# The last column of each state's scan: copied by VectorE instead of ScalarE

## The chip, the core and the metric

The kernel runs on one core of a Trainium2 chip. A core has five engines that run side by side, each with its own queue of instructions: TensorE (PE, matrix products), VectorE (DVE), ScalarE (ACT), GpSimd (POOL) and SyncE (SP, which starts transfers). They wait for each other through semaphores. An instruction that waits holds up everything behind it in its own queue. The metric is the time of one execution on the device in microseconds (us); lower is better.

## The reference

The input x has shape (2, 2048, 256): two sequences of 2048 tokens. Two blocks follow each other, each added to its input. The first is a Mamba block with a gated feed-forward part, the second a mixture of eight low-rank experts, two for each token. What matters here is the selective scan in the Mamba block. For each of 512 channels d and each of 16 states s:

```python
dA = jnp.exp(dt_t[..., None] * A)
h = h * dA + dt_t[..., None] * B_t[:, None, :] * x_t[..., None]
y = jnp.einsum('bds,bs->bd', h, C_t)
```

h starts at zero and runs on through all 2048 tokens. The output y goes through a gate and a projection. A kernel that cuts the tokens into chunks must hand h at the last token of a chunk to the same sequence's next chunk.

## The kernel before

The tokens are cut into 8 chunks of 256 for each of the 2 sequences, so there are 16 **steps**, written (chunk, sequence). The 512 channels lie on 128 partitions as 4 blocks. In a step the 16 **states** go round one after the other, and each state's scan has two **parts** of two channel blocks (a "pair" of scans, 128x256 each).

For a state s the engines do this:

- ScalarE makes the decays dA with four exponentials (L871) and, for most states, the weighted inputs bxT (L859). GpSimd makes bxT for states 4, 6 and 8 (L602).
- TensorE turns bxT into one of three PSUM banks psx (L1340), one bank for each pair. It must wait until the pair that used the bank three fills earlier has been scanned.
- VectorE scans: two instructions for each part (L1095). It reads dA and psx, starts from the column `state[:, b, j, s]`, and writes h, a ring of three states. The last two states, 14 and 15, have their decays in PSUM (L882) and their inputs in SBUF.
- GpSimd multiplies h by C into hC (L631), one instruction of 128x1024 for each state, after both parts.
- TensorE sums the states into psy (L1359).
- ScalarE copies the last column of h into `state` (L889), for the same sequence's next chunk. This is `keep_state`. A later scan that writes the same slot of the ring waits for it (`state_saved`).

Around these lies the rest of the network. `drive` sets the order on every engine: for each state s first `main(s, n, 0)`, then the stage work of turn s of other steps (`enter` and `ready` prepare the coming steps, `back` and `tail` finish earlier ones), then `main(s, n, 1)`. So up to five steps are in work at once, and VectorE's stage work (convolution taps L1059, softplus repair L1067 to L1073, sums out of PSUM L1111, L1133 and L1189, gates L1126, expert weights L1170, router L1149 to L1159) stands between the first and the second pair of a state, while a second pair and the next state's first pair follow each other directly. In `drive`:

```python
for s in range(S):
    if n:
        main(s, n, 0)
    for name in order[s] if s in order else order["else"]:
        ...
    if n:
        main(s, n, 1)
```

ScalarE issues `keep_state(s - 1, n)` in `main(s, n, 1)`, ahead of bxT and the decays of state s + 3, and `keep_state(15)` in the first turn of `back`.

Of the kernel before, what the change touches and what calls it, by code (L numbers as in the profile page):

```python
# [6 lines left out]
B, L, DM, DI, S, TAPS, DTR, HID = 2, 2048, 256, 512, 16, 4, 128, 1024  # L7
NE, RANK = 8, 128
P = 128
T = 256  # L10
# [10 lines left out]
HALVES = 2  # L21
PAIR = NJ // HALVES
FILLS = S * HALVES
# [34 lines left out]
def count(per_step, step, k):  # L58

    c, b = step  # L60
    value = c * (2 * per_step) + (per_step * b + k)
    return max(value, 0) if isinstance(value, int) else value
# [51 lines left out]
def ring(s):  # L114

    return s % 3 if s < S - 1 else 1
# [81 lines left out]
def mamba_moe(nc, x, params, w_in, w_x, w_dt, w_out, w_ff, w_fo, w_a, w_b, w_r, bc_scratch, cw_scratch, out):  # L198
    f32 = mybir.dt.float32
    ALU = mybir.AluOpType  # L200
    ACT = mybir.ActivationFunctionType
# [6 lines left out]
    with ctx:  # L208
        def sb(name, shape):
            return ctx.enter_context(nc.sbuf_tensor(name, shape, f32))  # L210
# [56 lines left out]
        h = sb("h", [P, 3, NJ, T])  # L267
        hC = sb("hC", [P, RC, NJ, T])
        state = sb("state", [P, B, NJ, S])
# [78 lines left out]
        exp_done, scan_done, state_saved = sem("exp_done"), sem("scan_done"), sem("state_saved")  # L348
# [341 lines left out]
        def _(act):  # L690
# [192 lines left out]
                                                scale=neg_a[:, j, s:s + 1])  # L883
                last.then_inc(direct_exp, 1)

            def keep_state(s, n):

                act.wait_ge(scan_done, count(FILLS, n, HALVES * (s + 1)))
                nc.scalar.activation(state[:, n[1], :, s:s + 1], h[:, ring(s), :, T - 1:T], ACT.Copy  # L889
                                     ).then_inc(state_saved, 1)  # L890

            def gate(i, m):

                act.wait_ge(filled_back, back_fill(f"G{i}", m))
# [2 lines left out]
            def main(s, n, part):  # L897
                if s + 1 in DIRECT:
                    decay_direct(s + 1, part, n)
                if part == 0 and s == 3:  # L900
                    act.wait_ge(yg_done, count(2, n, -2))
                    act.wait_ge(z0_filled, count(1, n, 1))
                    nc.scalar.activation(sz[:, n[1], 0, :], psb[:, :, :].rearrange("p k t -> p (k t)"), ACT.Copy
                                         ).then_inc(z0_copied, 1)
                if part == 1:
                    if s > 0:
                        keep_state(s - 1, n)
                    if s == 10:
                        act.wait_ge(z0_copied, count(1, n, 1))
                        act.wait_ge(z1_copied, count(1, n, 1))  # L910
                        nc.scalar.activation(sz[:, n[1]], sz[:, n[1]], ACT.Silu).then_inc(sz_done, 1)
                        if not is_first(n):
                            gate(1, prev(n))
                        use_log_exp()
                    made(s, n)

            def back(s, m):
                if s == 0:
                    keep_state(S - 1, m)
                if s in (3, 4):  # L920

                    i = s - 3
                    act.wait_ge(filled_back, back_fill(f"YG{i}", m))
                    nc.scalar.activation(yg[:, 2 * i:2 * i + 2, :], (psb, pst)[i][:, :, :], ACT.Copy).then_inc(yg_moved, 1)  # L924
                if s == 7:
                    act.wait_ge(stats[1], count(1, m, 1))
                    inv_std(2, mv[1][:, :, 1], m).then_inc(rstd_done[2], 1)
                    if not is_last(m):
                        mean_shift(1, m)
                        act.wait_ge(cw_done, count(1, m, 0))  # L930
                        normalise(1, nx, x1, vn_done)
                if s == 9:

                    act.wait_ge(filled_back, back_fill("vT", m))
                    act.wait_ge(filled_dt, count(len(DT_UNITS), m, 2 if is_late(m) else 2 * len(DT_UNITS) + 2))
                    act.wait_ge(cw_stored, count(16, m, 0))
                    for k in range(KM):
                        last = nc.scalar.activation(nT[:, k, :], psb[:, k, :], ACT.Identity, scale=pcol(C_LN2W + k),  # L938
                                                    bias=pcol(C_LN2B + k))
                    last.then_inc(vT_done, 1)  # L940
                if s == 10:
                    gate(0, m)
                    if is_last(m):
                        gate(1, m)
                        use_log_exp()
                if s == 15:
                    act.wait_ge(stats[2], count(1, m, 1))
                    inv_std(3, mv[2][:, :, 1], m).then_inc(rstd_done[3], 1)
                    if not is_last(m):
                        mean_shift(2, m)  # L950
                        act.wait_ge(filled_back, back_fill("vT", m))
                        normalise(2, nx, x2[:, m[1]], xe_done)
# [36 lines left out]
        def _(dve):  # L989
# [85 lines left out]
            def main(s, n, part):  # L1075
                b, r = n[1], ring(s)
                fill = HALVES * s + part
                if part == 0:
                    if s in DIRECT:
                        dve.wait_ge(direct_done, count(ND, n, s - DIRECT[0] + 1))  # L1080
                    else:
                        dve.wait_ge(exp_done, count(S - ND, n, s + 1))

                    dve.wait_ge(hc_done, count(S, n, ring_before(s) + 1))
                    dve.wait_ge(state_saved, count(S, n, ring_before(s) + 1))
                if s in DIRECT:
                    dve.wait_ge(direct_exp, count(HALVES * ND, n, fill - TURNED + 1))
                else:
                    dve.wait_ge(bx_filled, count(TURNED, n, fill + 1))
                for k in range(PAIR):  # L1090
                    j = PAIR * part + k
                    in_psum = psx[bx_bank(fill)][:, k, :]
                    decays, inputs = ((in_psum, direct_inputs(s)[:, j, :]) if s in DIRECT
                                      else (dA[:, s % RA, j, :], in_psum))
                    last = nc.vector.tensor_tensor_scan(h[:, r, j, :], decays, inputs, state[:, b, j, s:s + 1],  # L1095
                                                        ALU.mult, ALU.add)
                last.then_inc(scan_done, 1)

            def back(s, m):
                b = m[1]  # L1100
                if s == 2:

                    dve.wait_ge(y_summed, count(S, m, S))
                    dve.wait_ge(sz_done, count(1, m, 1))
                    for j in range(SUB):
                        nc.vector.tensor_tensor(ygt[:, j, :], psy[j][:, :], sz[:, b, j, :], ALU.mult).then_inc(yg_done, 1)
                if s == 6:

                    dve.wait_ge(filled_back, back_fill("op", m))
                    dve.wait_ge(xk_copied, count(16, m, 16))  # L1110
                    nc.vector.tensor_tensor(x1[:, :, :], xk[:, b], psb[:, :, :], ALU.add).then_inc(x1_done, 1)  # L1111
                    dve.wait_ge(x1_done, count(1, m, 1))
                    norm_stats(1, x1, "back", m)
                if s == 7 and is_last(m):
                    dve.wait_ge(cw_done, count(1, m, 0))
                    dve.wait_ge(rstd_done[2], count(1, m, 1))
                    normalise(1, nx, x1, vn_done)
                if s == 15 and is_last(m):
                    dve.wait_ge(filled_back, back_fill("vT", m))
                    dve.wait_ge(rstd_done[3], count(1, m, 1))  # L1120
                    normalise(2, nx, x2[:, b], xe_done)
                if s in (11, 12):
                    i = s - 11
                    dve.wait_ge(gate_done, count(2, m, i + 1))
                    dve.wait_ge(filled_back, back_fill(f"A{i}", m))
                    nc.vector.tensor_tensor(hg[:, 2 * i:2 * i + 2, :], hg[:, 2 * i:2 * i + 2, :],  # L1126
                                            up_bank(i, m)[:, :, :], ALU.mult).then_inc(hg_done, 1)
                if s == 14:

                    dve.wait_ge(filled_back, back_fill("fo", m))  # L1130
                    dve.wait_ge(x1x_done, count(1, m, 1))
                    dve.wait_ge(out_stored, count(16, m, -16))
                    nc.vector.tensor_tensor(x2[:, b], xb[:, :, :], psb[:, :, :], ALU.add).then_inc(x2_done, 1)  # L1133
                    dve.wait_ge(x2_done, count(1, m, 1))
                    norm_stats(2, x2[:, b], "back", m)
# [406 lines left out]
```

## Time and profile before

| | |
|---|---|
| three runs, median (lowest to highest) | 1285.68 us (1285.03 to 1286.23) |
| the profiled execution | 1286.74 us |
| its span, from the first instruction to the last | 1284.8 us |
| granted TensorE clock, mean of the span | 0.979 |
| PE, DVE, ACT, POOL busy | 93%, 77%, 85%, 79% of the span |

The busy share is an average over the span. In the opening and in the last stretch some engines have little to do; in between, TensorE's share is higher than 93%. An engine's idle time is shown with what released it. A wait for several semaphores is put down to the last one.

### The profile page before, as it was taken

To read this page: it belongs to the slowest core of one execution; us is meant where nothing else is said; L and a number is where in the kernel's file an instruction comes from. 1 tells how busy PE (TensorE), PEld (TensorE's weight loads), DVE (VectorE), ACT (ScalarE), POOL (GpSimd) and SP (SyncE) were. 2 spreads that over 40 slices of the span, in tenths; PEclk is the share of its full clock that TensorE was granted. 3 is DMA by queue.
4 is the path that set the end of the run, shared out by engine and by line. 5 is a ranking of instruction groups with operands and counts; after the bars stand their busy time and mean duration, and the time that the engine had idled before them with its cause. 6 is when DMAs were issued, how large, how long until landed. Compare 5 with 4: busy or idle time off the path is not lost.

```text
span 1284.8 us, 24309 instructions
## 1 busy us (share of the span) xinstructions
PE 1197.1 (93%) x7422; PEld 1029.2 (80%) x7422; DVE 995.6 (77%) x1800; ACT 1089.1 (85%) x2656; POOL 1019.4 (79%) x760
## 2 busy tenths in 40 slices
PE   5677989999999999999999999999999999998988
PEld 3466778888888888888888888888888888787876
DVE  2587987889797887879788887978889796887733
ACT  4888999899898989989898998989899998988621
POOL 2489798888888988888898888889888887888621
PEclk8797999999999999999999999999999999999999
DMA  2511102112221312222121222213121221203010
GB/s 69 199 58 52 65 19 105 46 52 90 67 92 34 100 43 64 79 68 91 42 94 43 69 72 69 92 36 98 43 75 67 68 83 53 87 36 99 17 50 17
DMA packets 33927, 86.83 MB, mean 68 GB/s; under 512 B 3592, under 2 KB 16512, under 8 KB 31360
## 3 DMA queue, kind: packets, MB, share of 16 engines
q1 hardware_dynamic: 33792, 85.20, 20.2%
q8 instruction: 64, 1.05, 0.3%
q14 instruction: 71, 0.58, 0.1%
HBM read 67.76 MB, written 4.84 MB: 57 GB/s over the span
## 4 chain that ended last, share of the span: by engine, by line
PE 67%; DVE 8%; issue 4%; ACT 2%; POOL 2%; DMA 2%; DVEq 0%; SPq 0%; ACTq 0%; POOLq 0%
PE psy L1359 11%; PE psx L1340 10%; PE pst L1220 8%; PE psb L1220 7%; PE psb L1214 6%; PE psf L1214 5%; PE pst L1214 4%; DVE h L1095 4%; PE psf L1308 2%; PE psf L1314 2%; PE psf L1258 2%; PE psf L1247 2%; PE psb L1314 2%; DVE acc L1059 2%; PE psb L1207 1%
## 5 line engine op out<-in xcount | busy, mean ns | idle before, releaser
L631 POOL TENSOR_TENSOR hC<-h,bC 128x1024 f32<-128x1024 f32 x256 | 604.5, 2368 | 126.1 <-DVE h L1095 116.8
L1095 DVE TENSOR_TENSOR_SCAN h<-dA,state,psx 128x256 f32<-128x256 f32 x896 | 597.2, 726 | 102.3 <-PE psx L1340 94.4
L871 ACT ACTIVATE dA<-dt,neg_a 128x256 f32<-128x256 f32 x896 | 380.1, 500 | 0.0
L1340 PE MATMUL psx<-ident,bxT 128*128 128x128 f32 x1792 | 270.5, 278 | 34.1 <-DVE h L1095 28.7
L1340 PEld LDWEIGHTS psx<-ident,bxT 128*128 128x128 f32 x1792 | 215.7, 143 | 74.4 <-issue 29.6
L1359 PE MATMUL psy<-ident,hC 128*128 128x128 f32 x2048 | 267.7, 274 | 3.9 <-POOL hC L631 3.9
L1359 PEld LDWEIGHTS psy<-ident,hC 128*128 128x128 f32 x2048 | 235.7, 142 | 10.6 <-POOL hC L631 4.7
L859 ACT ACTIVATE bxT<-uTs,BT 128x512 f32<-128x512 f32 x352 | 232.4, 715 | 5.9 <-PE psx L1340 3.1
L1220 PE MATMUL pst<-w_b_sb,cbc 128*128 128x256 f32 x480 | 110.8, 379 | 0.0
L1220 PEld LDWEIGHTS pst<-w_b_sb,cbc 128*128 128x128 f32 x480 | 90.1, 190 | 11.7
L882 ACT ACTIVATE psx<-dt,neg_a 128x256 f32<-128x256 f32 x128 | 55.3, 463 | 49.7 <-DVE h L1095 49.7
L602 POOL TENSOR_TENSOR bxT<-uTs,BT 128x1024 f32<-128x1024 f32 x48 | 91.2, 1899 | 4.4 <-PE psx L1340 4.3
L1214 PE MATMUL psb<-nT,w_ff_sb 128*128 128x256 f32 x376 | 91.7, 387 | 1.4 <-ACT nT L938 1.4
L1059 DVE SCALAR_TENSOR_TENSOR acc<-psf,par,acc 128x255 f32<-128x255 f32 (+1 forms) x180 | 73.9, 474 | 24.6 <-ACT halo L763 24.6
L1214 PEld LDWEIGHTS psb<-nT,w_ff_sb 128*128 128x128 f32 x376 | 68.9, 190 | 15.5 <-issue 5.7
L1214 PE MATMUL pst<-eT,w_a_sb 128*128 128x256 f32 x336 | 80.7, 384 | 0.0
L1214 PEld LDWEIGHTS pst<-eT,w_a_sb 128*128 128x128 f32 x336 | 62.6, 193 | 7.6
L1214 PE MATMUL psf<-uT,w_in_sb 128*128 128x256 f32 x240 | 60.7, 397 | 4.1 <-ACT uT L748 2.1
L1220 PE MATMUL psb<-w_out_sb,yg 128*128 128x256 f32 x256 | 62.0, 385 | 2.0 <-ACT yg L924 2.0
L1220 PE MATMUL psb<-w_fo_sb,yg 128*128 128x256 f32 x256 | 60.4, 379 | 0.0
L590 POOL TENSOR_TENSOR dt<-dt,sp_l 128x1024 f32<-128x1024 f32 x16 | 37.8, 2360 | 28.0 <-DVE sp_l L1073 28.0
L1095 DVE TENSOR_TENSOR_SCAN h<-psx,state,sp_e 128x256 f32<-128x256 f32 x64 | 44.2, 735 | 17.1 <-ACT state L889 12.8
(178 smaller groups left out, 1894.5 us busy)
## 6 DMA issues: line engine op xcount, KB each, us to landing
bC<-bc_scratch SPq DMA_DIRECT2D x64, 512.0 KB, 4.0
cbc<-cw_scratch SPq DMA_DIRECT2D x15, 1024.0 KB, 4.7
uk<-sp_l SPq DMA_DIRECT2D x16, 512.0 KB, 6.3
xf<-in_x SPq DMA_DIRECT2D x16, 256.0 KB, 2.7
xk<-xn SPq DMA_DIRECT2D x16, 256.0 KB, 4.3
un<-bc_scratch SPq DMA_DIRECT2D x16, 256.0 KB, 4.1
xb<-in_x SPq DMA_DIRECT2D x16, 256.0 KB, 5.3
out<-x SPq DMA_DIRECT2D x16, 256.0 KB, 2.2
```

The costliest lines, as they stand in the source:

```text
L602: nc.gpsimd.tensor_tensor(bxT[:, s % RX], uTs[:, n[1]], BT[:, n[1], :, s:s + 1].to_broadcast([P, SUB, DI]), ALU.mult).then_inc(bxT_pool, 1)
L631: nc.gpsimd.tensor_tensor(hC[:, s % RC], h[:, ring(s)], bC[:, g % RINGG, s % G:s % G + 1, :].to_broadcast([P, NJ, T]), ALU.mult).then_inc( ...
L859: last = nc.scalar.activation(bxT[:, s % RX, j, :], uTs[:, n[1], j, :], ACT.Copy, scale=BT[:, n[1], j, s:s + 1])
L871: last = nc.scalar.activation(dA[:, s % RA, j, :], dt[:, n[1], j, :], ACT.Exp, scale=neg_a[:, j, s:s + 1])
L882: last = nc.scalar.activation(psx[bx_bank(fill)][:, k, :], dt[:, n[1], j, :], ACT.Exp, scale=neg_a[:, j, s:s + 1])
L1059: nc.vector.scalar_tensor_tensor(out=acc[:, j, tap:], in0=x_bank(i, m)[:, j % 2, 0:T - tap], scalar=pcol(C_CONVW + j * TAPS + k), in1=acc[ ...
L1095: last = nc.vector.tensor_tensor_scan(h[:, r, j, :], decays, inputs, state[:, b, j, s:s + 1], ALU.mult, ALU.add)
L1214: last = mm(dst[:, i, :], w[:, k, c:c + P], rhs[:, k, :], start=k == 0, stop=k == kt - 1)
L1220: last = mm(dst[:, j, :], lhs[:, k, j * P:(j + 1) * P], w[:, k, :], start=k == 0, stop=k == kt - 1)
L1314: last = mm(dst[:, :, :].rearrange("p k t -> p (k t)"), uT[:, b, k, j * P:(j + 1) * P], w_in_sb[:, k, DI:2 * DI], start=k == 0, stop=k == ...
L1340: last = nc.tensor.transpose(psx[bx_bank(fill)][:, k, j * P:(j + 1) * P], bxT[:, s % RX, j, c:c + P], ident[:, :])
L1359: last = mm(psy[j][:, i * P:(i + 1) * P], hC[:, s % RC, i, j * P:(j + 1) * P], ident[:, :], is_transpose=True, start=False, stop=s == S - ...
```

## The change

ScalarE no longer copies the last column. VectorE does, with `tensor_copy` in place of an activation: the copy of state s - 1 stands behind the first pair of scans of state s, and that of state 15 in the first turn of `back`, behind the first pair of state 0 of the next step. It waits on VectorE's own semaphore `scan_done` for the second pair of its state. The scans still wait for `state_saved`, which VectorE now raises itself.

```diff
 # ScalarE
-            def keep_state(s, n):
-
-                act.wait_ge(scan_done, count(FILLS, n, HALVES * (s + 1)))
-                nc.scalar.activation(state[:, n[1], :, s:s + 1], h[:, ring(s), :, T - 1:T], ACT.Copy
-                                     ).then_inc(state_saved, 1)
...
                 if part == 1:
-                    if s > 0:
-                        keep_state(s - 1, n)
...
             def back(s, m):
-                if s == 0:
-                    keep_state(S - 1, m)
...
 # VectorE, main
                 last.then_inc(scan_done, 1)
+                if part == 0 and s > 0:
+                    keep_state(s - 1, n)
+
+            def keep_state(s, n):
+
+                dve.wait_ge(scan_done, count(FILLS, n, HALVES * (s + 1)))
+                nc.vector.tensor_copy(state[:, n[1], :, s:s + 1], h[:, ring(s), :, T - 1:T]).then_inc(state_saved, 1)
 
             def back(s, m):
                 b = m[1]
+                if s == 0:
+                    keep_state(S - 1, m)
```

VectorE's queue before, from the second pair of state 7 to the second pair of state 8 (the listing calls the scans SCALAR_TENSOR_TENSOR; psx0 to psx2 are the banks, and [waits ...] are the semaphores an instruction waits for):

```order
L1095 SCALAR_TENSOR_TENSOR h<-dA,state,psx0 128x256 [waits bx_filled]
L1095 SCALAR_TENSOR_TENSOR h<-dA,state,psx0 128x256
L1095 SCALAR_TENSOR_TENSOR h<-dA,state,psx1 128x256 [waits state_saved,bx_filled,hc_done,exp_done]
L1095 SCALAR_TENSOR_TENSOR h<-dA,state,psx1 128x256
L1170 TENSOR_TENSOR cbc<-cbc,psb 128x512 [waits filled_tail]
L1067 SCALAR_TENSOR_TENSOR sp_l<-sp_l,ln_one,sp_e 128x1024 [waits sp_ln]
L1069 TENSOR_SCALAR sp_e<-sp_e 128x1024
L1095 SCALAR_TENSOR_TENSOR h<-dA,state,psx2 128x256 [waits bx_filled]
```

The same place in the changed kernel, whose lines are numbered up to ten lower:

```order
L1085 SCALAR_TENSOR_TENSOR h<-dA,state,psx0 128x256 [waits bx_filled]
L1085 SCALAR_TENSOR_TENSOR h<-dA,state,psx0 128x256
L1085 SCALAR_TENSOR_TENSOR h<-dA,state,psx1 128x256 [waits state_saved,bx_filled,hc_done,exp_done]
L1085 SCALAR_TENSOR_TENSOR h<-dA,state,psx1 128x256
L1094 COPY state<-h 128x4 [waits scan_done]
L1169 TENSOR_TENSOR cbc<-cbc,psb 128x512 [waits filled_tail]
L1057 SCALAR_TENSOR_TENSOR sp_l<-sp_l,ln_one,sp_e 128x1024 [waits sp_ln]
L1059 TENSOR_SCALAR sp_e<-sp_e 128x1024
L1085 SCALAR_TENSOR_TENSOR h<-dA,state,psx2 128x256 [waits bx_filled]
```

The copy of state 7 now stands between state 8's first pair and the stage work of that turn; the rest keeps its order.

ScalarE's queue before, in turns 7 and 8 of a step (sz is a half of the gate, copied out of PSUM):

```order
L889 ACTIVATE state<-h 128x4 [waits scan_done]
L859 ACTIVATE bxT<-uTs,BT 128x512 [waits bx_filled]
L859 ACTIVATE bxT<-uTs,BT 128x512
L871 ACTIVATE dA<-dt,neg_a 128x256 [waits scan_done]
L871 ACTIVATE dA<-dt,neg_a 128x256 x3
L818 ACTIVATE sz<-psf 128x512 [waits filled_dt,yg_done]
```

The same place in the changed kernel:

```order
L859 ACTIVATE bxT<-uTs,BT 128x512 [waits bx_filled]
L859 ACTIVATE bxT<-uTs,BT 128x512
L871 ACTIVATE dA<-dt,neg_a 128x256 [waits scan_done]
L871 ACTIVATE dA<-dt,neg_a 128x256 x3
L818 ACTIVATE sz<-psf 128x512 [waits filled_dt,yg_done]
```

The copy and its wait for the scans ahead of bxT are gone; the decays behind bxT wait for the same scans as before.

## Rows read from the trace of the kernel before

**Rows 1.** The page's first part: busy us (share of the span) xinstructions.

```profile
PE 1197.1 (93%) x7422; PEld 1029.2 (80%) x7422; DVE 995.6 (77%) x1800; ACT 1089.1 (85%) x2656; POOL 1019.4 (79%) x760
```

**Rows 2.** Busy us in five stretches: PE, PEld, DVE, ACT, POOL; clock, DMA, GB/s.

```profile
48.65:119.00 70.35, 50.65 (x291) 40.26 (x288) 52.97 (x86) 64.76 (x154) 56.31 (x34) 0.84 0.16 50
119.00:188.90 69.90, 61.60 (x387) 51.79 (x387) 58.61 (x101) 62.98 (x155) 61.12 (x35) 0.94 0.17 54
188.90:1084.76 895.86, 878.76 (x5568) 761.38 (x5568) 738.57 (x1328) 809.97 (x1991) 763.26 (x563) 1.00 0.21 68
1084.76:1154.66 69.90, 66.90 (x436) 59.17 (x436) 55.81 (x96) 62.56 (x153) 57.81 (x37) 1.00 0.22 69
1154.66:1224.30 69.64, 63.11 (x415) 56.57 (x416) 53.27 (x92) 48.27 (x121) 53.22 (x35) 0.98 0.19 58
```

**Rows 3.** VectorE's waits, 188.90 to 1084.76: us in total, times, longest.

```profile
DVE h L1095 <- PE psx L1340: 69.8, 47, 3.3
DVE yg L1126 <- PE psb L1214: 26.3, 13, 2.3
DVE x L1111 <- PE psb L1220: 14.9, 12, 1.2
DVE acc L1059 <- ACT halo L763: 12.5, 12, 1.2
DVE h L1095 <- ACT state L889: 10.4, 12, 0.9
DVE x L1189 <- PE pst L1220: 8.8, 12, 0.8
```

**Rows 4.** TensorE's waits in the same stretch.

```profile
PE psx L1340 <- DVE h L1095: 9.3, 12, 0.8
...
PE psx L1340 <- ACT bxT L859: 2.5, 2, 1.3
```

**Rows 5.** One line's instructions: xcount, ns min/median/max, first and last start.

```profile
L889 ACT ACTIVATE state<-h x256: 192/195/243, 60.3 to 1224.3; 128x4 f32<-128x4 f32 x128
```

**Rows 6.** The same view of four VectorE lines.

```profile
L1154 DVE TENSOR_TENSOR lgm<-lg,mx x16: 174/386/1761, 201.8 to 1267.9; 128x16 f32<-128x16 f32 x16
...
L1159 DVE RECIPROCAL rden<-den x16: 166/166/167, 207.5 to 1273.0; 128x2 f32<-128x2 f32 x16
...
L1069 DVE TENSOR_SCALAR sp_e<-sp_e x16: 679/680/687, 35.0 to 1122.2; 128x1024 f32<-128x1024 f32 x16
...
L1073 DVE TENSOR_TENSOR sp_l<-sp_l,sp_e x16: 1225/1898/2328, 35.7 to 1126.0; 128x1024 f32<-128x1024 f32 x16
```

**Rows 7.** Timeline, VectorE then GpSimd: start us, us, engine, line, operation, [idle before].

```profile
1162.92 1.76 DVE L1154 TENSOR_TENSOR lgm<-lg,mx 128x16 f32<-128x16 f32 x1
...
1162.29 2.35 POOL L631 TENSOR_TENSOR hC<-h,bC 128x1024 f32<-128x1024 f32 x1
```

**Rows 8.** Timeline of VectorE in the step from 638.59 us.

```profile
645.11 2.66 DVE L1095 TENSOR_TENSOR_SCAN h<-dA,state,psx 128x256 f32<-128x256 f32 x4 [1.23 <-PE psx L1340]
...
649.45 0.18 DVE L1154 TENSOR_TENSOR lgm<-lg,mx 128x16 f32<-128x16 f32 x1
649.55 5.45 DVE L1095 TENSOR_TENSOR_SCAN h<-dA,state,psx 128x256 f32<-128x256 f32 x8
...
676.38 1.85 DVE L1067 SCALAR_TENSOR_TENSOR sp_l<-sp_l,ln_one,sp_e 128x1024 f32<-128x1024 f32 x1
...
678.75 2.65 DVE L1095 TENSOR_TENSOR_SCAN h<-dA,state,psx 128x256 f32<-128x256 f32 x4
```

**Rows 9.** Timeline of GpSimd in the same step.

```profile
647.01 2.38 POOL L631 TENSOR_TENSOR hC<-h,bC 128x1024 f32<-128x1024 f32 x1
...
654.88 2.36 POOL L631 TENSOR_TENSOR hC<-h,bC 128x1024 f32<-128x1024 f32 x1
...
674.77 2.38 POOL L631 TENSOR_TENSOR hC<-h,bC 128x1024 f32<-128x1024 f32 x1 [0.34 <-DVE h L1095]
680.36 2.36 POOL L631 TENSOR_TENSOR hC<-h,bC 128x1024 f32<-128x1024 f32 x1 [3.21 <-DVE h L1095]
```

## The prediction

> **What bounds the kernel now.** I read the page's busy line first. It shows TensorE busy for 93% of the span and GpSimd, ScalarE and VectorE for 77 to 85% [rows 1]. Then the windows, cut where the first scan of a step starts. There are 16 steps, of 16 states each. The 12 steps from 188.90 to 1084.76 us take 895.86 us, so 74.7 us each. TensorE is busy for 878.76 of that (98%), VectorE for 738.57 (61.5 a step), ScalarE for 809.97 and GpSimd for 763.26 (63.6 a step) [rows 2]. So in the steady part TensorE sets the pace, at full clock, and VectorE has 74.7 - 61.5 = 13.2 us of idle time in a step. The waits say where that idle time is: VectorE waits for TensorE's psx banks (69.8 us over the 12 steps), for the gate halves, out_proj and the expert sum (26.3, 14.9 and 8.8), for ScalarE's halo (12.5) and for ScalarE's saved state (10.4) [rows 3]. TensorE in turn waits little: 9.3 us for scans and 2.5 us for ScalarE's bxT [rows 4].
>
> **What is removed.** ScalarE loses 256 copies of 195 ns [rows 5]. It is not the bound, and the only one who waits for them is the first scan of state 15, 12 times in 12 steps, 0.87 us each [rows 3]. That wait goes. What is late next there is the sum L1189, which waits for TensorE [rows 3], so the end of the step does not come earlier. ScalarE's decays still wait for the scans of the state before. The stalls of TensorE on bxT, 2.5 us in all [rows 4], are the most that a freer ScalarE can give back. I take zero for the removal, with 2.5 us as its bound.
>
> **What is added.** VectorE gets 256 copies of 128x4, SBUF to SBUF, 16 a step, each behind the first pair of scans of the next state. The wait on the own scan costs nothing: that scan ended a whole pair of scans (half of 2.66 us for four, 1.33 us) earlier. What the copy itself costs no row shows, because VectorE has no copy in this trace. The nearest rows disagree:
>
> Cheap end: the reciprocal L1159, one SBUF input, 128x2, takes 166 to 167 ns in all 16 cases [rows 6], and a short instruction of this kind takes 0.10 us of the queue: L1154 starts at 649.45 and the next scan at 649.55 [rows 8]. So 16 x 0.10 = 1.6 us a step, inside 13.2 us of idle time.
>
> Dear end: L1154, a 128x16 subtraction with two SBUF inputs, takes 174 ns at least and up to 1761 ns [rows 6]. In that longest case it starts at 1162.92 and ends at 1164.68, and GpSimd's product, begun at 1162.29, ends at 1164.64 [rows 7]. The subtraction stood until GpSimd's instruction was over. L1067 does the same: begun at 676.38 for 1.85 us, while GpSimd's product runs from 674.77 to 677.15 [rows 8, 9], which is 0.77 us of standing and 1.08 of work. So a VectorE instruction that needs a second way into SBUF waits for whatever GpSimd is running.
>
> Is the copy of that sort? L1069, with one SBUF input and an SBUF output, does 1024 elements in 0.68 us, where L1073 with two inputs needs 1.225 us at best [rows 6]. So it handles two elements at a time, which a single way in at L1073's pace would not feed. It never meets GpSimd in this trace: it stands between L1067 and the next scans, when GpSimd idles until 680.36 for a scan [rows 8, 9]. I take the copy to be of L1069's sort, with L1154's wait, and not of the reciprocal's.
>
> A rule speaks against this change here. The Trainium skill's page SBUF — State Buffer, section Who interferes with whom, says that copies and tensor_scalar can run in a two-port mode, that the second port pair is shared with GpSimd, and that whichever issues first holds it for its whole instruction while the other blocks. Its list of such operations is copy, cast and tensor_scalar; the reciprocal is not in it. By that rule the sum below holds, and by the reciprocal's row alone it would be 1286. The waits in [rows 7] agree with the rule for two inputs; that a copy behaves so no run here shows yet.
>
> **The price of a wait.** The copy stands behind the first pair of state s, and at that moment GpSimd is usually inside the product of state s-1, which began when that state's second pair ended. Read in one step (from 638.59 us): the four scans from 678.75 end at 681.41 while GpSimd's product ends at 682.72: 1.32 us left. Those from 645.11 end at 647.77 and the product at 649.39: 1.6 us. The eight from 649.55 end at 655.00 and the product at 657.24: 2.2 us [rows 8, 9]. Over the 16 places of that step, read in the same way, the rests are 0, 0.65, 1.61, 0, 2.24, 0.35, 0.82, 1.25, 1.26, 1.32, 0.03, 0.61, 2.10, 1.43, 1.24 and 0.25, together 15.2 us. When VectorE becomes the slower one, most places turn into the plain case of 1.25 (product of 2.37 less the pair of 1.33, and a start that lags a little), which makes 16 x 1.25 = 20. I take 17.5.
>
> The sum of VectorE for one steady step: 61.5 busy, less 1.8 of waits for GpSimd that are in it already and that the copy ahead now takes over (0.77 at L1067, 0.8 at L1073, 0.2 at L1154, median less minimum in [rows 6] for the last), plus 17.5 of waiting, plus 1.6 for the copies: 78.8. That is more than the 74.7 that TensorE needs, so VectorE becomes the bound. Its other idle time does not all go. Waits behind the copy in the queue (for the gate halves, out_proj, halo, expert sum and half of the psx waits) are covered by the standing time; the rest of the psx waits, about half of 69.8 / 12 = 5.8, stays: 3. So 81.8 us a step, 7.1 more, and 12 x 7.1 = 85 us. The four steps at the ends, by the same sum from their own busy time [rows 2]: the first 53.0 + 20.3 = 73.3 against 70.4, the second 78.9 against 69.9, the last two 76.1 and 73.6 against 69.9 and 69.6, together 22 us. The profiled execution took 1286.74 us; plus 107 that is 1394, and on the median of 1285.68, which is 1.06 lower, **1393 us**.
>
> What is queued behind the waiting copy: on VectorE the stage work of that state and the second pair of scans. For that pair wait GpSimd's product of the state and TensorE's next bank of psx, so TensorE is held up too.
>
> **Rivals.**
> 1. *The copy is of the reciprocal's sort.* It takes 1.6 us of 13.2 idle a step, nobody waits, and TensorE stays the bound. For it: L1159 never waited, and a copy of four elements has little use for two at a time. Against it: L1069's pace. Between 2.5 us off for the bxT stalls and some 3 us more where TensorE already waits for a scan (0.8 us at each of 12 step ends [rows 4], to which two copies add 0.2): 1283 to 1289, likeliest 1286, no change.
> 2. *The wait is there but hides.* With 15.2 us of rests and no idle time left, a step takes 61.5 - 1.8 + 15.2 + 1.6 = 76.5, 1.8 more: 12 x 1.8 plus some 5 at the ends, 1312 us. This is the low end of my own case.
> 3. *GpSimd's next instruction goes first.* If the copy stands until GpSimd has nothing left that is ready, the two engines overlap only in the first pair of each state: 63.6 of GpSimd, 1.6 of copies and 61.5 - 1.8 - 16 x 1.33 = 38.4 of the other VectorE work make 103.6 a step, 29 more, over 15 steps 1720 us at the far end. Half of it, 1500, if only some places have a next instruction ready. For it: GpSimd is busy for 63.6 of 74.7 us, so often something is ready. Against it: at L1067 and L1154 the waiting instruction went on as soon as the running one ended, though nothing was ready behind it there [rows 7 to 9], so the trace does not decide.
>
> The decision between 1 and the forecast falls at a wait of 13.2 / 16, about 0.7 us for each copy beyond its 0.1: under that VectorE's idle time holds it, above it the time grows.
>
> **How the numbers follow.** Forecast with its own range of 1312 to 1470 (high end: rests of 20 and 6 us of idle time left, 61.5 - 1.8 + 20 + 1.6 + 6 = 87.3, which is 12.6 more over 15 steps, 1475): 0.69, rival 2 in it. Rival 3: 0.14. Rival 1: 0.17, of which 0.05 faster, 0.09 no change, 0.03 a little slower. The likeliest is 1393. Leaving out rival 3 and the edges, 1284 to 1470 holds 8 in 10; it reaches to rival 1 because that is as likely as rival 3 and nearer. A measurement of this kernel can tell about 0.2% from no change, so faster 0.05, same 0.09, slower 0.86.
>
> **What would show it.** The copy's line in the profile after: a minimum near 0.1 and a median near 1.2 us shows the wait; a median under 0.2 us makes the forecast wrong and rival 1 right. In the windows, VectorE's busy time should rise from 61.5 to near 78 a step and TensorE's busy share fall from 98% to about 90%, with scans as what TensorE waits for. GpSimd's product should keep its 2.37 us. In the timelines each copy should end with GpSimd's running instruction; if it ends with the one after, it is rival 3. The wait of state 15 for ScalarE should be gone in every case.

## The result, and the profile after

The changed kernel takes 1385.92 us (median of 4 runs, 1382.47 to 1388.15), the kernel before beside it 1285.95 us (4 runs, 1285.03 to 1288.75). The ratio is 1.0778, with a 95% interval of 1.0752 to 1.0804: slower by 100 us, where the forecast was 1393 us. The profiled execution took 1388.15 us, with a span of 1386.2 us; the span is 101.4 us longer than before.

The page's first part for the changed kernel, with columns as in [rows 1]:

```profile
PE 1221.3 (88%) x7422; PEld 1040.1 (75%) x7422; DVE 1257.6 (91%) x2056; ACT 1066.4 (77%) x2400; POOL 1018.9 (74%) x760
```

VectorE has 256 instructions more and 262 us more of busy time, ScalarE 256 fewer and 22.7 us less. GpSimd's busy time is that of [rows 1]. VectorE is now the busiest engine. The chain of work that ended last, first by engine and then by line, says the same:

```profile
DVE 41%; PE 39%; issue 12%; ACT 4%; DVEq 1%; POOL 0%; ACTq 0%
DVE h L1085 20%; DVE state L1094 10%; PE psx L1339 6%; PE psb L1213 6%; PE psy L1358 5%; PE pst L1213 3%; DVE acc L1049 3%; PE psb L1219 3%; PE psf L1213 3%; PE pst L1219 2%; DVE bn L1002 2%; PE psf L1246 2%; ACT dA L871 1%; PE psf L1257 1%; DVE cbc L1169 1%
```

The new copy, `state` L1094, holds 10% of the chain. Next come the rows of single lines (name, count, ns min/median/max, first and last start): the copy, GpSimd's product, and three VectorE lines with two SBUF inputs, of which L1063 and L1153 are L1073 and L1154 of [rows 6], and L1057 is L1067 of [rows 8].

```profile
L1094 DVE COPY state<-h x256: 139/1354/2347, 54.8 to 1319.9; 128x4 f32<-128x4 f32 x128
...
L631 POOL TENSOR_TENSOR hC<-h,bC x256: 2339/2362/2393, 59.8 to 1319.9; 128x1024 f32<-128x1024 f32 x128
...
L1057 DVE SCALAR_TENSOR_TENSOR sp_l<-sp_l,ln_one,sp_e x16: 1271/1273/1284, 33.9 to 1208.5; 128x1024 f32<-128x1024 f32 x16
...
L1063 DVE TENSOR_TENSOR sp_l<-sp_l,sp_e x16: 1210/1212/1224, 35.8 to 1214.7; 128x1024 f32<-128x1024 f32 x16
...
L1153 DVE TENSOR_TENSOR lgm<-lg,mx x16: 174/175/641, 220.8 to 1366.6; 128x16 f32<-128x16 f32 x16
```

A copy of four elements takes 139 ns at best and 1354 in the median, ten times as long. GpSimd's product is as long as before. The three lines with two inputs no longer wait, one L1153 of 641 ns apart: the copy ahead of them has already stood until GpSimd's instruction was over. The timeline of one stretch shows it, VectorE first and then GpSimd (start us, us, engine, line, operation, [idle before]):

```profile
727.68 1.36 DVE L1085 TENSOR_TENSOR_SCAN h<-dA,state,psx 128x256 f32<-128x256 f32 x2
728.96 1.36 DVE L1094 COPY state<-h 128x4 f32<-128x4 f32 x1
730.23 0.68 DVE L1169 TENSOR_TENSOR cbc<-cbc,psb 128x512 f32<-128x512 f32 x1
730.83 1.27 DVE L1057 SCALAR_TENSOR_TENSOR sp_l<-sp_l,ln_one,sp_e 128x1024 f32<-128x1024 f32 x1
...
735.20 1.42 DVE L1094 COPY state<-h 128x4 f32<-128x4 f32 x1
...
740.83 0.14 DVE L1094 COPY state<-h 128x4 f32<-128x4 f32 x1
...
727.92 2.37 POOL L631 TENSOR_TENSOR hC<-h,bC 128x1024 f32<-128x1024 f32 x1 [1.62 <-DVE h L1085]
734.23 2.35 POOL L631 TENSOR_TENSOR hC<-h,bC 128x1024 f32<-128x1024 f32 x1 [3.94 <-DVE h L1085]
...
740.74 0.21 POOL L582 TENSOR_TENSOR acc<-acc,edge 128x12 f32<-128x12 f32 x1
```

The first copy starts at 728.96 and ends at 730.32; the product runs from 727.92 to 730.29. The second ends at 736.62, the product at 736.58. The third meets only a 0.21 us instruction and takes 0.14.

Where the 101.4 us are is read from the windows, cut as in [rows 2], with a sixth stretch for what follows the last scan:

```profile
48.71:126.14 77.43, 53.23 (x290) 41.78 (x288) 68.21 (x101) 64.46 (x141) 58.12 (x34) 0.79 0.15 46
126.14:206.26 80.12, 65.39 (x386) 54.91 (x386) 74.58 (x117) 62.46 (x140) 59.50 (x34) 0.88 0.15 47
206.26:1170.02 963.76, 887.98 (x5568) 761.68 (x5568) 932.36 (x1521) 791.29 (x1797) 762.53 (x562) 1.00 0.19 63
1170.02:1246.20 76.18, 67.60 (x436) 59.19 (x436) 75.14 (x111) 61.70 (x138) 57.81 (x37) 1.00 0.20 63
1246.20:1319.80 73.60, 64.51 (x418) 56.88 (x418) 70.52 (x108) 46.15 (x103) 53.18 (x35) 0.98 0.16 55
1319.80:1386.20 66.40, 55.39 (x238) 47.06 (x238) 19.96 (x57) 12.52 (x27) 12.04 (x28) 0.86 0.09 31
```

The 12 steady steps take 963.76 us instead of 895.86: 67.9 us, or 5.66 a step (80.3 against 74.7). VectorE is busy for 932.36 / 12 = 77.7 us of each and idle for 2.6; TensorE's share falls from 98% to 92%. The four steps at the ends take 7.1, 10.2, 6.3 and 4.0 us more, together 27.5. What follows the last scan takes 66.40 us instead of 60.50, so 5.9 more. The same stretch of the kernel before:

```profile
1224.30:1284.80 60.50, 48.83 (x244) 41.45 (x242) 19.66 (x55) 12.65 (x28) 12.04 (x28) 1.00 0.10 34
```

VectorE, ScalarE and GpSimd are as busy there as before; TensorE is busy for 55.39 us instead of 48.83, at a granted clock of 0.86 instead of 1.00. So these 5.9 us go with the clock and not with standing copies. The stretch up to the first scan gives the last 0.1.

What VectorE and TensorE wait for in the steady stretch (engine, line, releaser: us in total, times, longest):

```profile
DVE h L1085 <- PE psx L1339: 25.6, 23, 2.2
DVE x L1110 <- PE psb L1219: 1.4, 1, 1.4
...
PE psf L1213 <- DVE acc L1049: 21.3, 12, 2.0
PE psf L1313 <- DVE acc L1049: 17.8, 12, 1.5
PE psx L1339 <- DVE h L1085: 15.8, 25, 1.3
PE psb L1206 <- DVE cbc L1169: 8.5, 12, 0.7
```

VectorE's waits for the gate halves, out_proj, the expert sum, the halo and the saved state [rows 3] have shrunk to 1.4 us or are gone. Its waits for psx fell from 69.8 to 25.6 us. TensorE, which waited 9.3 us for scans [rows 4], now waits 63 us for VectorE's results in these four rows alone.

### The profile page after: what moved, and what is told of

Read it like the earlier page. It is cut to its first block, busy times and chain, and to the rows that moved or that the text cites. A ratio compares the mean times of both kernels' runs of the same rounds, so it can differ in the third digit from the quotient of the medians.

```text
span 1386.2 us, 24413 instructions
## 1 busy us (share of the span) xinstructions
PE 1221.3 (88%) x7422; PEld 1040.1 (75%) x7422; DVE 1257.6 (91%) x2056; ACT 1066.4 (77%) x2400; POOL 1018.9 (74%) x760
## 4 chain that ended last, share of the span: by engine, by line
DVE 41%; PE 39%; issue 12%; ACT 4%; DVEq 1%; POOL 0%; ACTq 0%
DVE h L1085 20%; DVE state L1094 10%; PE psx L1339 6%; PE psb L1213 6%; PE psy L1358 5%; PE pst L1213 3%; DVE acc L1049 3%; PE psb L1219 3%; PE psf L1213 3%; PE pst L1219 2%; DVE bn L1002 2%; PE psf L1246 2%; ACT dA L871 1%; PE psf L1257 1%; DVE cbc L1169 1%
## 5 line engine op out<-in xcount | busy, mean ns | idle before, releaser
L1094 DVE COPY state<-h 128x4 f32<-128x4 f32 x256 | 320.8, 1253 | 0.0
L1213 PE MATMUL psf<-uT,w_in_sb 128*128 128x256 f32 x240 | 63.7, 412 | 29.8 <-DVE acc L1049 27.7
L1213 PEld LDWEIGHTS psb<-nT,w_ff_sb 128*128 128x128 f32 x376 | 69.0, 190 | 17.7 <-issue 5.3
L1213 PEld LDWEIGHTS psf<-uT,w_in_sb 128*128 128x128 f32 x240 | 46.4, 203 | 40.1 <-DVE acc L1049 31.1
L757 ACT ACTIVATE acc<-psf,par 128x256 f32<-128x256 f32 x60 | 30.6, 559 | 45.5 <-PE psf L1213 45.4
```

The source lines that it names most:

```text
L1094: nc.vector.tensor_copy(state[:, n[1], :, s:s + 1], h[:, ring(s), :, T - 1:T]).then_inc(state_saved, 1)
L1213: last = mm(dst[:, i, :], w[:, k, c:c + P], rhs[:, k, :], start=k == 0, stop=k == kt - 1)
```

## The experiments

The theory: the copy needs the way into SBUF that GpSimd holds, and stands until GpSimd's running instruction is over; VectorE, which had 13 us of idle time a step, becomes the bound. The rivals: the loss comes from ScalarE's side or from the hand-over; or the copy's own length and its place in the queue cost the time; or a waiting copy lets GpSimd's next instruction go ahead. "Ratio" below is the time over that of the kernel before, run beside it, with its 95% interval in brackets; "copies' total" is the busy time of all copies in one profile.

**The same column by another operation.** The reduction has one input and one output of the same size and stands in the same place.

```diff
-nc.vector.tensor_copy(state[:, n[1], :, s:s + 1], h[:, ring(s), :, T - 1:T]).then_inc(state_saved, 1)
+nc.vector.reduce_max(state[:, n[1], :, s], h[:, ring(s), :, T - 1:T], X).then_inc(state_saved, 1)
```

> The changed kernel with one difference: the last column is kept by a maximum over one element (a reduction, 128x4 out) in place of the copy, at the same place in VectorE's queue, with the same wait on the own scans, the same bytes and the same semaphore. Theory (the copy stands until GpSimd's running instruction is over, because it needs a second way into SBUF, and a reduction does not): 0.14 to 0.17 us each as the other small reductions take, 16 x 0.1 = 1.6 us a step inside VectorE's idle time, 1284 to 1290 us. Rival (the place in the queue, the wait on the own scans or the strided column is what costs): about as long as the changed kernel, 1370 to 1390 us, and near 1.3 us for each reduction.

Measured: 1285.91 us, ratio 1.0004 (0.998 to 1.0028). The row of its line:

```profile
L1094 DVE TENSOR_REDUCE state<-h x256: 123/134/160, 52.7 to 1222.5; 128x4 f32<-128x4 f32 x128
```

None of the 256 reductions waits, though 237 of them begin and end inside a GpSimd instruction, and the whole loss is gone. So neither the move off ScalarE, nor the place in VectorE's queue, nor one more short instruction a state costs anything that can be measured. The Trainium skill's page SBUF — State Buffer, section Who interferes with whom, says that a reduction never contends with GpSimd on this chip, while a copy can: these 160 ns at most, against 2347 for the copy, agree.

**Half of the copies.** VectorE copies the odd states, ScalarE keeps the even ones.

```diff
+                if part == 0 and s > 0 and s % 2 == 0:
+                    keep_state(s - 1, n)
```

> VectorE copies the last column of the odd states only, 8 a step, and ScalarE that of the even states as before. Theory (each copy stands some 1.3 us in VectorE's queue, but only what exceeds its 13.2 us of idle time a step lengthens the step): 8 x 1.3 = 10.4 us, under 13.2, so most of it hides: 1290 to 1315 us. Rival (each copy delays the step by its own wait, in proportion): half of the 100 us, 1330 to 1340 us.

Measured: 1310.64 us, ratio 1.0205 (1.0162 to 1.0248). Copies' total 159.3 us.

```profile
L1107 DVE COPY state<-h x128: 140/1294/2942, 59.2 to 1246.5; 128x4 f32<-128x4 f32 x128
```

Half of the copies stand about as long each as all of them did, but cost a quarter of the loss. The first half falls partly on VectorE's idle time. Not all of it does: 159.3 us is 10 a step, less than the 13.2 that were idle, and the kernel is still 2% slower. The sum of the idle time is not at hand where the copies stand: in its steady steps VectorE is still idle for 6.7 us each, while TensorE now waits 8.5 us over the 12 steps for VectorE's expert weights (L1182 here), for which it did not wait before. Two of the 128 copies stood longer than a whole product lasts, 2.94 and 2.72 us: they began inside one product and ended with the next.

**The kernel before with a useless copy on VectorE.** ScalarE keeps all its copies; VectorE copies the same column into a tile that nobody reads.

```diff
+                if part == 0 and s > 0:
+                    extra_copy(s - 1, n)
...
+                nc.vector.tensor_copy(spare[:, :, :], h[:, ring(s), :, T - 1:T]).then_inc(spare_done, 1)
```

> The kernel before, in which ScalarE keeps the last columns, and besides VectorE copies each of them once more into a tile that nobody reads, at the place where the changed kernel has its copy. Theory (all of the loss is the copy's standing on VectorE, ScalarE's freed time is worth nothing): within 5 us of the changed kernel, 1380 to 1392 us. Rival (part of the loss comes from ScalarE's side: its queue without the wait for the scans runs ahead and takes PSUM or buffers at another time): well under the changed kernel, 1330 to 1370 us.

Measured: 1384.09 us, ratio 1.0774 (1.0739 to 1.0809), copies' total 318.8 us. The whole loss comes with the copy alone, so it has nothing to do with who waits for the state.

**The kernel before without any copy.** It leaves out the hand-over of the state from one chunk of the sequence to the next, with its waits.

```diff
-                    if s > 0:
-                        keep_state(s - 1, n)
...
-                    dve.wait_ge(state_saved, count(S, n, ring_before(s) + 1))
```

> The kernel before without the copy of the last column and the waits for it: nothing is handed on between chunks (every chunk's scan starts at zero). This is the removal alone. Theory (ScalarE is not the bound, and what it gives back is at most the 2.5 us of TensorE's stalls on bxT): 1281 to 1287 us. Rival (the wait of state 15's scan for ScalarE, 0.87 us at each step's end, is on the path): 16 x 0.9 less, 1270 to 1274 us.

Measured: 1283.12 us, ratio 0.9964 (0.9937 to 0.999). Taking the copies off ScalarE, at no price elsewhere, is worth 0.4% (0.1 to 0.6).

**The copy right behind its own second pair of scans.** At that moment GpSimd's product of the same state gets ready too; both wait for that scan.

```diff
-                if part == 0 and s > 0:
-                    keep_state(s - 1, n)
+                if part == 1:
+                    keep_state(s, n)
```

> The changed kernel with the copy of state s directly behind state s's own second pair of scans, so that the copy and GpSimd's product of that state wait for the same scans and become ready together. Theory with GpSimd first: each copy stands for a whole product, 2.37 us, so VectorE has 61.5 + 16 x 2.4 = 100 us a step, 1600 to 1700 us. Theory with the copy first where GpSimd is idle: about half of the places are free and cost 0.15 to 0.25 us (the copy must wait for the scan's end), the other half stand as in the changed kernel, 1300 to 1350 us. Rival (the place does not matter): 1380 to 1390 us.

Measured in a single run: 1324.72 us, beside 1286.31 for the kernel before. Copies' total 156.1 us.

```profile
L1094 DVE COPY state<-h x256: 170/174/2192, 50.5 to 1262.3; 128x4 f32<-128x4 f32 x128
```

140 of the 256 take less than 0.3 us. In 96 of these GpSimd was idle: the copy starts some 0.05 to 0.2 us before the product and goes first. Most of the others meet only a short GpSimd instruction. The other 116 stand over 0.3 us: there GpSimd was still inside an instruction ahead of the product when the scan ended.

**The copy one pair later**, ahead of the second pair of the next state instead of behind its first, so that the stage work stands in between.

```diff
+                if part == 1 and s > 0:
+                    keep_state(s - 1, n)
                 if part == 0:
...
-                if part == 0 and s > 0:
-                    keep_state(s - 1, n)
```

> The changed kernel with the copy of state s - 1 later: behind the stage work of turn s, directly ahead of the second pair of state s. Theory (the copy stands for what is left of GpSimd's running instruction): stage work of 0.6 to 3.1 us in eleven turns lets the product run out meanwhile, some 9 to 10 us of standing in a step are left at the turns without stage work, while the waits of L1067 and L1073 come back: 61.5 + 10 + 1.6 = 73 and some idle time, 1290 to 1325 us. Rival (a copy costs its 1.25 us wherever it stands): 1375 to 1395 us.

Measured: 1316.87 us, ratio 1.0239 (1.02 to 1.0278), copies' total 230.2 us.

```profile
L1094 DVE COPY state<-h x256: 138/948/2370, 54.0 to 1252.6; 128x4 f32<-128x4 f32 x128
```

Fewer copies are held there: 156 stand over 0.3 us, where 218 do in the changed kernel. Those that stand do so for about as long, 1.36 us in the median in both. Two thirds of the loss were a matter of the place.

**The column by an operation with two inputs**, both of them that column.

```diff
+                last_col = h[:, ring(s), :, T - 1:T]
+                nc.vector.tensor_tensor(state[:, n[1], :, s:s + 1], last_col, last_col, ALU.max).then_inc(state_saved, 1)
```

> The changed kernel with a maximum of the last column with itself (tensor_tensor, both inputs in SBUF, 128x4) in place of the copy. Theory (what stands is any VectorE instruction that reads SBUF by a second way, as L1154 does): 1.3 us each as the copy, 1375 to 1392 us. Rival (only copies stand, because they also write by a second way): 0.1 us each, 1284 to 1290 us as with the reduction.

Measured: 1380.78 us, ratio 1.0745 (1.0705 to 1.0786), copies' total 321.0 us.

```profile
L1095 DVE TENSOR_TENSOR state<-h x256: 136/1348/2346, 53.8 to 1313.8; 128x4 f32<-128x4 f32 x128
```

It behaves as the copy does, to within 10 ns in the minimum, the median and the maximum. So the copy has the wait that the prediction read off the two-input lines of [rows 6, 7].

**GpSimd's product in four pieces of 128x256**, in the changed kernel and in the kernel before. If a copy waits only for the running instruction, shorter instructions should shorten the wait.

```diff
+                    for j in range(NJ):
+                        last = nc.gpsimd.tensor_tensor(hC[:, s % RC, j, :], h[:, ring(s), j, :],
+                                                       bC[:, g % RINGG, s % G, :], ALU.mult)
+                    last.then_inc(hc_done, 1)
```

> The changed kernel (copies on VectorE) with GpSimd's product of a state cut into four instructions of 128x256. From the rows of other sizes (399 ns for 128x128, 1277 for 128x512, 2368 for 128x1024) each should take about 0.73 us, 16 x 0.4 = 6 us more of GpSimd in a step, which has 11 us idle. Theory (a copy stands for the rest of the one instruction that GpSimd is running): at most 0.7 us a copy, some 0.3 to 0.4 on average, 16 x 0.45 = 7 us a step, within VectorE's idle time: 1286 to 1305 us. Rival (a copy stands until GpSimd's work that is ready is done, so four short ones cost what the long one does): 1380 us or more.

> The same cut of GpSimd's product in the kernel before, where ScalarE copies: what the cut costs by itself. Theory and rival alike: GpSimd's 6 us more a step fit into its idle time and the first quarter does not start earlier, 1284 to 1295 us.

Measured: 1403.80 us, ratio 1.0907 (1.0859 to 1.0954), for the changed kernel, and 1335.87 us, ratio 1.0396 (1.0347 to 1.0444), for the kernel before. Both forecasts of the theory, 1286 to 1305 and 1284 to 1295, were wrong. The product's group in the kernel before, cut into pieces (count | busy us, mean ns | idle before):

```profile
L632 POOL TENSOR_TENSOR hC<-h,bC 128x256 f32<-128x256 f32 x1024 | 729.4, 749 | 76.2 <-DVE h L1096 74.7
```

Four pieces of 749 ns make 3.0 us, where the whole product takes 2.37 [rows 7]. GpSimd gets 125 us more work (729.4 us where the product had 604.5), and that alone makes the kernel before 52 us slower. On top of that the copies cost 68 us, where they cost 100 with whole products. The rest of the miss is in the copies of the changed kernel:

```profile
L1095 DVE COPY state<-h x256: 138/415/6426, 52.9 to 1334.8; 128x4 f32<-128x4 f32 x128
...
565.91 1.30 POOL L640 TENSOR_TENSOR xb<-x,xb 128x512 f32<-128x512 f32 x1
...
566.64 3.35 DVE L1095 COPY state<-h 128x4 f32<-128x4 f32 x1
...
567.15 2.81 POOL L632 TENSOR_TENSOR hC<-h,bC 128x256 f32<-128x256 f32 x4
...
569.90 0.67 DVE L1170 TENSOR_TENSOR cbc<-cbc,psb 128x512 f32<-128x512 f32 x1
```

The median fell to 0.42 us as the theory has it. But this copy starts while GpSimd adds `xb`, and is passed over when `xb` ends and three times more: it ends with the fourth piece, at 569.99. 30 of the 256 copies stand longer than 2.4 us, most of them until the fifth or sixth end of a GpSimd instruction, and 23 of the 30 get in only where no GpSimd instruction follows within 0.3 us. That is the third rival of the prediction. In the changed kernel with whole products no copy stands longer than 2.35 us.

**What ends such a run of pieces.** The same kernel with a wait ahead of the second, third and fourth piece: in the first case for something that is met already, in the second for the end of the piece before, so that GpSimd pauses.

```diff
+                        if j > 0:
+                            pool.wait_ge(scan_done, count(FILLS, n, HALVES * (s + 1)))
```

```diff
+                        if j > 0:
+                            pool.wait_ge(part_done, count((NJ - 1) * S, n, (NJ - 1) * s + j))
...
+                        if j < NJ - 1:
+                            last.then_inc(part_done, 1)
```

> The kernel of the change with GpSimd's product in four pieces of 128x256, as in the run before, and a wait ahead of the second, third and fourth piece for the scans of the same state, which the product has waited for already, so that it never holds anything up. Theory A: a waiting VectorE copy is passed over where GpSimd's next instruction is already issued when the running one ends, and a wait in GpSimd's queue, even one that is met, opens the place: then no copy stands through more than two GpSimd instructions, the copies' total falls from 237 us to 130 to 170, and the time from 1404 us to 1340-1375. Theory B: what decides is only whether GpSimd leaves a real pause between two instructions, and a wait that is met leaves none: then copies of 5 to 7 pieces stay (25 to 35 of them), the total stays at 225-245 and the time at 1395-1410.

> The kernel of the change with GpSimd's product in four pieces of 128x256, where each of the last three pieces waits until the piece before it has ended, so that GpSimd pauses between pieces. Theory A and theory B both: no copy stands through more than one piece behind the running instruction, median of the copies about 0.4 us, total 110 to 160 us. The pauses make the product itself longer (0.05 to 0.15 us each, 2.4 to 7 us a step), so the time stays above the kernel before: 1340-1400. If copies of 5 to 7 pieces are still there, both theories are wrong, and GpSimd keeps its way in across a pause.

Measured: 1394.39 us, ratio 1.0871 (1.082 to 1.0923), with the wait that is met, and 1383.52 us, ratio 1.0757 (1.072 to 1.0794), with the pause. The copies of the one and of the other:

```profile
L1097 DVE COPY state<-h x256: 134/450/5343, 53.1 to 1324.3; 128x4 f32<-128x4 f32 x128
```

```profile
L1100 DVE COPY state<-h x256: 135/444/2365, 52.5 to 1316.5; 128x4 f32<-128x4 f32 x128
```

With the wait that is met, 28 copies still stand longer than 2.4 us, and their total is 228.6 us: theory A of that expectation falls, and theory B's count and total come out (its time of 1395 to 1410 just missed). With a pause none does, and the total is 144.7. The time does not follow: GpSimd with its pauses is busy for 1189 us, and 46% of the chain that ended last is its own.

The copies' total and the time, side by side, from the profiles and runs above; every row keeps GpSimd's product whole:

| kernel | copies' total, us | time, us |
|---|---|---|
| reduction in the copy's place | 34.2 | 1285.9 |
| copy behind its own pair (one run) | 156.1 | 1324.7 |
| odd states alone | 159.3 | 1310.6 |
| one pair later | 230.2 | 1316.9 |
| useless copy in the kernel before | 318.8 | 1384.1 |
| the change | 320.8 | 1385.9 |
| two inputs | 321.0 | 1380.8 |

With the same total the time is the same within the intervals of the ratios (1.0774, 1.0778, 1.0745), whoever keeps the state. Between the ends it depends on where the copies stand.

## Why the prediction was right

**The bound.** That TensorE bounds the steady part with some 13 us of VectorE's time idle holds: the reduction puts 34.2 us of work into that idle time and the time does not move.

**The removal.** Taken at zero with a bound of 2.5 us. The kernel without any copy is 0.4% faster (0.1 to 0.6), so 4.6 us (1.3 to 8.1): the bound lies inside this interval, the middle above it. In the profiles its 12 steady steps take 892.5 us where the kernel before takes 895.9, and with the reduction 894.6. So the removal may have been taken a little too low, which does not matter beside 100 us. The wait for ScalarE's state is gone, as every case had it.

**The sort of the copy.** This was the step with the decision in it, and no row of before showed the copy. The reciprocal's row gave 1286, the two-input rows gave 1393. That row held more than the prediction took from it: 14 of the 16 reciprocals begin and end inside one of GpSimd's products, so the trace of before already showed that a line of that sort does not wait. (The 0.10 us taken for it was read off L1154, which has two inputs, at a moment when no product ran.) The reduction in its place and the two-input operation in its place show both answers on the chip: 134 and 1348 ns in the median, 1285.9 and 1380.8 us. What put the copy on the dear side was the pace of L1069 [rows 6], an argument on speed alone; the experiments show that the wait is there, and what in the copy makes it need GpSimd's way was not tried.

**The size of the wait.** Taken at 17.5 us a step, plus 1.6 for the copies themselves. The 192 copies of the steady steps are busy for 237.3 us, 19.8 a step, about 2 us of overlap with their neighbours in it. The 20 of the plain case, worked out as 16 x 1.25, is what this comes to, 1.25 being the mean of one copy (320.8 / 256). The rests summed to 15.2 (two that were read as 0 are 0.18 and 0.45 by the timeline), and 17.5 was a choice between the two. The 1.6 was counted once too often: a copy ends 0.03 us after GpSimd's instruction, so its own work lies inside the wait. Without the overlap the copies add 77.7 - 61.5 + 1.5 = 17.7 us a step to VectorE, where 17.5 + 1.6 = 19.1 was taken. The credit of 1.8 for waits already paid, the 1.5 in this sum, was a little too large: 1.85 to 1.27 at L1067 (0.58 where 0.77 was taken), 1.898 to 1.212 at L1073 and 0.386 to 0.175 at L1154, each by the median or the row that was read. The net of VectorE's busy time is 77.7 us a step, where 78.8 was forecast, and its idle time 2.6, where 3 was.

**The steps at the ends and the tail.** 22 us forecast, 27.5 measured. The second, fifteenth and sixteenth steps came out as worked out (10.2, 6.3 and 4.0 against 9.0, 6.2 and 4.0). The first took 7.1 us more instead of 2.9: the sum left VectorE 3 us of idle time there as elsewhere, and it is idle for 77.4 - 68.2 = 9.2. The 5.9 us behind the last scan, which go with the lower clock, were not forecast at all. So the steady part was 17 us too dear (85 against 68) and the rest 11 us too cheap. These errors cancel in part, and that is luck: the profiled execution took 1388.15 us where 1394 was forecast for it, and the steady part alone was off by some three times as much.

**The rivals.** The first (the reciprocal's sort) is refuted by the copy's median. The second (it hides) gave 1312, with no idle time left to VectorE. Half of the copies, and the copy one pair later, come out near that number but not in that way: there VectorE is idle for 6.7 and 3.1 us of a steady step. The third (GpSimd's next instruction goes first) does not happen in the changed kernel: 237 of the 256 copies see exactly one GpSimd instruction end while they stand and 19 none (an end within 0.02 us of the copy's start is not counted), also where the next product starts at once. It does happen with the product in pieces. The trace of before could not decide it, as the prediction said, and its price, 1500 us and more, stays untried.

## What to carry to other kernels

Before a short VectorE instruction is put beside a busy GpSimd, ask by which operation it is done: the same four elements took 134 ns as a reduction and 1354 ns as a copy, and 256 of them made 0 or 100 us. If it must be a copy, price it by what is left of GpSimd's instruction at its place, and look for a place where GpSimd is idle or nearly done. A sum of idle time is not a cover: 10 us of standing a step cost 2% under 13 us of idle time.

## What was not expected of the hardware

In the changed kernel every copy that waits is let in after the running GpSimd instruction. In the one with odd states alone, 2 of 128 were passed over by one whole product, and with the product cut some 30 of 256 by several pieces of 0.7 us, up to 6.4 us. A wait in GpSimd's queue that is met already changes nothing (28 against 30 long copies), a pause ends it (none). Why products that follow one another at once nearly always let the copy in, and some runs of pieces do not, stays open. In the kernel before with the product cut, a two-input VectorE line with 1.27 us of work has a median of 4.18 us:

```profile
L1068 DVE SCALAR_TENSOR_TENSOR sp_l<-sp_l,ln_one,sp_e x16: 1285/4183/4339, 32.9 to 1162.9; 128x1024 f32<-128x1024 f32 x16
```

The Trainium skill's page SBUF — State Buffer, section Who interferes with whom, says that whichever issues first keeps the shared way for its whole instruction; the changed kernel agrees, and these long waits, which began before three and more of the GpSimd instructions that went ahead of them, do not.

Cutting GpSimd's product is not free: 128x1024 takes 2.37 us and 128x256 takes 0.75, so by these two an estimate of (4 x 0.749 - 2.363) / 3 = 0.21 us goes with each instruction.

The stretch behind the last scan ran at a granted clock of 0.86, where that of the kernel before has 1.00 (the two levels are 1.2 and 2.4 GHz). It is 0.88 in the kernel with two inputs and in the one with the useless copy, and 1.00 with the reduction. It would be easy to say that the clock falls where VectorE holds TensorE up, but the kernel without any copy contradicts it:

```profile
1218.42:1281.39 62.97, 52.63 (x244) 44.89 (x242) 19.74 (x56) 12.52 (x27) 12.07 (x28) 0.92 0.09 32
```

Nothing was added to VectorE there, and the stretch still ran at 0.92 and took 62.97 us where the kernel before took 60.50. What makes the clock fall was not tried.
